# Moving the row variances and scales of a batch behind the queries' low part on VectorE

## The chip, the cores and the metric

The kernel runs on one core of a Trainium2 chip. The time is device microseconds of one execution; the figure compared is the median of the runs shown. In tables and rows PE is TensorE (PEld its weight loads), DVE is VectorE, ACT is ScalarE, POOL is GpSimd, and SP is SyncE, which issues the DMAs.

## What is computed

Two layers of cross attention and a feed-forward mixture of experts, on 4 batches of 512 rows of 256 values, with a context of 4 x 1024 rows of 192. The change touches only the layer norm inside the attention phase, which stands twice in the program (names that begin with `L0a_` and `L1a_`).

```python
def _layernorm(x, axis=-1, eps=1e-05):
    m = jnp.mean(x, axis=axis, keepdims=True)
    v = jnp.var(x, axis=axis, keepdims=True)
    return (x - m) / jnp.sqrt(v + eps)
...
        q = (x @ w_q).reshape(B, Sq, HEADS, DIM_HEAD).transpose(0, 2, 1, 3)
        k = (context @ w_k).reshape(B, Skv, HEADS, DIM_HEAD).transpose(0, 2, 1, 3)
        v = (context @ w_v).reshape(B, Skv, HEADS, DIM_HEAD).transpose(0, 2, 1, 3)
        sim = jnp.einsum('bhid,bhjd->bhij', q, k) * SCALE
        attn = jax.nn.softmax(sim, axis=-1)
        out = jnp.einsum('bhij,bhjd->bhid', attn, v)
        out = out.transpose(0, 2, 1, 3).reshape(B, Sq, INNER)
        return out @ w_o + b_o
...
    x = x + _L0_xattn_ref(_layernorm(x, axis=-1), ctx_768, L0_xattn_w_q, L0_xattn_w_k, L0_xattn_w_v, L0_xattn_w_o, L0_xattn_b_o)
    x = x + _L0_ffn_ref(_layernorm(x, axis=-1), L0_ffn_gate_weight, ...)
```

## The kernel before

An attention phase is 32 segments (`SEGMENTS`), one for each pair of heads of each batch: 8 pairs (`HP`), 4 batches. Segment i takes the exponentials and the product with the values of its own pair; in the same stretch it finishes the pair before it (row sums, normalisation, output product) and prepares the next ones (queries and scores' row maxima of i+1, keys of i+2). Every engine has its own list of instructions, written out by hand in `segment(i)` of that engine, and semaphores tie the lists together. Nothing is reordered by a scheduler, so the order of the code is the order on the engine.

One segment on each engine, in its order:

- TensorE: `transpose_max(i)` (line L802, the first instruction of a segment, which I use as its start), `queries(i+1)`, eight `qk` blocks with quarters of `project_values` between them, `output(i-1)`, then four times `score(i+1, qt)` (L796) with `pv` matmuls (L833) as filling and the keys of i+2 behind the second, and `total(i)` (L845). The third quarter of `project_values` waits for the semaphore `olo`. `score` 1 to 3 and `transpose_max` wait for `max`.
- VectorE: low part of the keys (L521); in segments with i % 8 = 0 or 1 the row statistics (L566); reciprocal of the row sums (L535, PSUM to SBUF), its product with the output (L538), high part (L544) and low part (L548) of the normalised output, of which the last gives `olo`; high part (L504) and low part (L509) of the next queries; in some segments a low part of the rows (L604); two additions of the output to `xres` (L558), four row maxima (L530) which give `max`, with low keys between them.
- GpSimd: `L0a_psums<-L0a_psums,L0a_probs` (L326), 14 sums over the keys' tiles of the exponentials in each segment, both operands in SBUF; low parts of weights (L307, L312) and context (L334).
- ScalarE: exponentials (L400), values (L388), once per batch the square root of the variances (L406, waits for `var`), the normalised rows (L415, waits for `scale`), high parts.

The layer norm of the rows of the next batch, and of the rows that are finished, is spread over the segments of a batch by the step i % 8: statistics in steps 0 and 1, the variances in step 2 (`ROOT`, `variance(b)`, L578 to L583), part of the scales in step 3 (`INNER`, L590 to L592) and the rest in step 4 (`OUTER`, L596 to L598). All of these work on tiles of 128 x 4 or 128 x 8 values in SBUF. L578 to L580 have no wait between them; from L581 on each waits for the one before it (the function `link`).

Of the kernel before, what the change touches and what calls it, by code (L numbers as in the profile page):

```python
# [46 lines left out]
def build(nc, x, ctx_top, ctx_bot, layer_in, out):  # L47
# [6 lines left out]
    with stack:  # L54
# [29 lines left out]
        def bank(n, width=BANK):  # L84
            return psum[:, n * BANK:n * BANK + width]
# [6 lines left out]
        def attention_phase(tag, weights, value_weights, bias, xres, prefetch, source=None, again=False, keep=False, clear=()):  # L92

            with scope() as s:
# [29 lines left out]
                with nc.Block() as block:  # L124
# [38 lines left out]
                    NEXT_STATS, LAST_STATS, ROOT, INNER, OUTER, BIAS = 0, 1, 2, 3, 4, 7  # L163
# [17 lines left out]
                    def columns_of(b):  # L181

                        used = [column for _, column in batches_of(b)] if b >= 0 else [0]
                        return slice(min(used), max(used) + QT)
# [313 lines left out]
                    def _(dve):  # L498
# [7 lines left out]
                        def low_queries(i, heads=(0, 1)):  # L506
                            for h in heads:
                                dve.wait_ge(sem["qhi"], 2 * i + h + 1)
                                last = nc.vector.tensor_tensor(q_lm[0:DH, i % 2, h, :], bank(PLACE["Q"])[HEAD[h], :],  # L509
                                                               q_hh[HEAD[h], i % 2, h, :], ALU.subtract)  # L510
                            if 1 in heads:
                                last.then_inc(sem["qlo"], 1)
# [47 lines left out]
                        def statistics(b, step):  # L560

                            c, column = (b + 1, 0) if step == NEXT_STATS else (b - 1, QT)
                            if step == LAST_STATS:
                                dve.wait_ge(sem["added"], BEFORE + 2 * (b * HP - 1) + 2)
                            for t in range(QT):
                                nc.vector.bn_stats(stats[:, column + t, :], xres[:, c * QT + t, :]).then_inc(sem["stat"], 1)  # L566
                            dve.wait_ge(sem["stat"], counted_stats(b, step))
# [3 lines left out]
                        def link(b, n, ins):  # L571
                            ins.then_inc(sem["link"], 1)
                            dve.wait_ge(sem["link"], LINKS * (b + 1) + n)

                        def variance(b):
                            c = columns_of(b)
                            me, se, mo, so = (stats[:, c, i] for i in (1, 2, 4, 5))
                            nc.vector.tensor_tensor(total_of[:, c], me, mo, ALU.add).then_inc(sem["link"], 1)  # L578
                            nc.vector.tensor_tensor(var[:, c], se, so, ALU.add).then_inc(sem["link"], 1)
                            link(b, 3, nc.vector.tensor_tensor(dif[:, c], me, mo, ALU.subtract))  # L580
                            link(b, 4, nc.vector.scalar_tensor_tensor(dif[:, c], dif[:, c], DIM / 4.0, dif[:, c], ALU.mult, ALU.mult))  # L581
                            link(b, 5, nc.vector.tensor_tensor(var[:, c], var[:, c], dif[:, c], ALU.add))
                            nc.vector.tensor_scalar(var[:, c], var[:, c], 1.0 / DIM, EPS, ALU.mult, ALU.add).then_inc(sem["var"], 1)  # L583

                        def inner_scales(b):
                            c = columns_of(b)
                            dve.wait_ge(sem["sqrt"], b + 2)
                            if b > 0:
                                dve.wait_ge(sem["xn"], 2 * len([i for i in GROUPS if i <= b * HP + INNER]) + 2)
                            link(b, 6, nc.vector.reciprocal(rstd[:, c], std[:, c]))  # L590
                            link(b, 7, nc.vector.tensor_tensor(dif[:, c], var[:, c], rstd[:, c], ALU.mult))
                            link(b, 8, nc.vector.tensor_tensor(dif[:, c], dif[:, c], rstd[:, c], ALU.mult))  # L592

                        def outer_scales(b):
                            c = columns_of(b)
                            link(b, 9, nc.vector.tensor_scalar(dif[:, c], dif[:, c], -0.5, 1.5, ALU.mult, ALU.add))  # L596
                            link(b, 10, nc.vector.tensor_tensor(rstd[:, c], rstd[:, c], dif[:, c], ALU.mult))
                            link(b, 11, nc.vector.scalar_tensor_tensor(shift[:, c], total_of[:, c], -0.5, rstd[:, c], ALU.mult, ALU.mult))  # L598
                            dve.sem_inc(sem["scale"], 1)
# [27 lines left out]
                        def segment(i):  # L627
                            if i + 1 < SEGMENTS:
                                low_keys(i + 1, 1)
                            b, step = divmod(i, HP)  # L630
                            if step == NEXT_STATS and b + 1 < BATCH:
                                if b == 0 and source is not None:
                                    dve.wait_ge(sem["x1"], 16)
                                statistics(b, step)
                            if step == LAST_STATS and b > 0:
                                statistics(b, step)
                            if step == ROOT:
                                variance(b)
                            if step == INNER:
                                inner_scales(b)  # L640
                            if step == OUTER:
                                outer_scales(b)
                            if i == 0:
                                add_bias(0)
                            if step == BIAS and b + 1 < BATCH:
                                add_bias(b + 1)
                            if i > 0:
                                normalise(i - 1)
                            if i > 0:
                                high_output(i - 1)  # L650
                                low_output(i - 1)
                            if i + 1 < SEGMENTS:
                                high_queries(i + 1)
                                low_queries(i + 1)
                            if i > 0:
                                if i in GROUPS:
                                    low_rows(number(i), GROUPS[i][0], PLACE["XT"])
                                add_output(i - 1)
                            if i + 1 < SEGMENTS:
                                for qt in range(QT):  # L660
                                    maximum(i + 1, qt)
                                    if qt in (1, 2) and i + 2 < SEGMENTS:
                                        low_keys(i + 2, 0, (qt - 1,))
# [1100 lines left out]
```

## Time and profile before

| what | value |
|---|---|
| median of 3 runs (2613.11 to 2613.93) | 2613.51 us |
| the profiled execution: time, span | 2618.82 us, 2616.9 us |
| TensorE busy | 2520.7 us, 96% of the span |
| VectorE busy | 2091.2 us, 80% |
| GpSimd busy | 1482.1 us, 57% |
| ScalarE busy | 1246.1 us, 48% |
| mean granted TensorE clock | 0.985 of full speed |

The profile is one execution with an instruction record for each engine. The profiled execution took 2618.82 us, 1.9 us more than its span, and 5.3 us more than the median of the three runs.

### The profile page before, as it was taken

To read this page: it belongs to the slowest core of one execution; us is meant where nothing else is said; L and a number is where in the kernel's file an instruction comes from. 1 tells how busy PE (TensorE), PEld (TensorE's weight loads), DVE (VectorE), ACT (ScalarE), POOL (GpSimd) and SP (SyncE) were. 2 spreads that over 40 slices of the span, in tenths; PEclk is the share of its full clock that TensorE was granted. 3 is DMA by queue.
4 is the path that set the end of the run, shared out by engine and by line. 5 is a ranking of instruction groups with operands and counts; after the bars stand their busy time and mean duration, and the time that the engine had idled before them with its cause. 6 is when DMAs were issued, how large, how long until landed. Compare 5 with 4: busy or idle time off the path is not lost. (4 is left out here: it accounts for less than half of the span.)

```text
span 2616.9 us, 37958 instructions
## 1 busy us (share of the span) xinstructions
PE 2520.7 (96%) x13304; PEld 1776.5 (68%) x13304; DVE 2091.2 (80%) x2602; ACT 1246.1 (48%) x1774; POOL 1482.1 (57%) x1124
## 2 busy tenths in 40 slices
PE   8999999999999889999999899999999999998795
PEld 6666565656665678888888766666666665656684
DVE  7888888888888487777777788888888888866695
ACT  5555555555554323333333355455555454533393
POOL 5878777877777311111111187687878777760345
PEclk9999999999999999999999999999999999999897
DMA  4122212222221200000000121222131222115112
GB/s 147 45 59 53 63 45 58 63 49 50 63 51 41 72 19 24 24 24 24 24 24 18 47 75 45 55 61 59 45 79 45 59 53 55 45 29 235 47 54 88
DMA packets 118648, 145.09 MB, mean 55 GB/s; under 512 B 63856, under 2 KB 80112, under 8 KB 117488
## 3 DMA queue, kind: packets, MB, share of 16 engines
q1 hardware_dynamic: 113664, 136.10, 19.3%
q0 software_dynamic: 1536, 4.20, 0.5%
q10 hardware_dynamic: 3312, 3.02, 0.3%
q8 instruction: 81, 1.33, 0.2%
q14 instruction: 55, 0.45, 0.1%
HBM read 80.93 MB, written 11.80 MB: 35 GB/s over the span
## 5 line engine op out<-in xcount | busy, mean ns | idle before, releaser
L326 POOL TENSOR_TENSOR L1a_psums<-L1a_psums,L1a_probs 128x512 f32<-128x512 f32 x384 | 479.1, 1293 | 0.0
L326 POOL TENSOR_TENSOR L0a_psums<-L0a_psums,L0a_probs 128x512 f32<-128x512 f32 x384 | 478.8, 1289 | 0.0
L530 DVE TENSOR_REDUCE L1a_row_max<-psum 128x2 f32<-128x2048 f32 x128 | 293.6, 2293 | 59.2 <-PE psum L796 58.9
L530 DVE TENSOR_REDUCE L0a_row_max<-psum 128x2 f32<-128x2048 f32 x128 | 293.5, 2293 | 57.7 <-PE psum L796 57.2
L400 ACT ACTIVATE L0a_probs<-psum 128x1024 f32<-128x1024 f32 x256 | 251.6, 1027 | 105.9 <-PE psum L819 105.7
L400 ACT ACTIVATE L1a_probs<-psum 128x1024 f32<-128x1024 f32 x256 | 251.6, 1027 | 105.1 <-PE psum L819 104.9
L1168 DVE SCALAR_TENSOR_TENSOR xres<-psum,L0e_weights_of,xres 128x256 f32<-128x256 f32 x544 | 225.6, 478 | 22.6 <-PE psum L1379 21.7
L833 PE MATMUL psum<-L1a_probs,L1a_v 128*64 128x512 f32 x1024 | 240.5, 601 | 0.0
L833 PE MATMUL psum<-L0a_probs,L0a_v 128*64 128x512 f32 x1024 | 240.4, 601 | 0.0
L1365 PE MATMUL psum<-xnT_hi,L0e_w_hi 128*128 128x512 f32 x544 | 215.0, 395 | 9.4 <-DVE L0e_hid L1176 9.4
L1365 PE MATMUL psum<-xnT_lo,L0e_w_hi 128*128 128x512 f32 x544 | 214.6, 394 | 0.0
L1365 PE MATMUL psum<-xnT_hi,L0e_w_lo 128*128 128x512 f32 x544 | 213.1, 392 | 0.0
L818 PE MATMUL psum<-L0a_q_hh,L0a_k_st 128*128 128x512 f32 x512 | 204.4, 399 | 1.4 <-ACT L0a_probs L400 0.9
L818 PE MATMUL psum<-L1a_q_hh,L1a_k_st 128*128 128x512 f32 x512 | 204.3, 399 | 1.4 <-ACT L1a_probs L400 0.9
L819 PE MATMUL psum<-L1a_q_lm,L1a_k_hs 65*128 65x512 f32 x512 | 203.1, 397 | 0.0
L819 PE MATMUL psum<-L0a_q_lm,L0a_k_hs 65*128 65x512 f32 x512 | 203.0, 397 | 0.0
L1113 ACT ACTIVATE L0e_act_g<-psum 128x512 f32<-128x512 f32 x136 | 81.3, 598 | 243.4 <-PE psum L1365 243.4
L558 DVE TENSOR_TENSOR xres<-psum,xres 128x512 f32<-128x512 f32 x128 | 88.6, 692 | 114.9 <-PE psum L708 113.8
L1176 DVE TENSOR_TENSOR L0e_hid<-psum,L0e_act_g 128x512 f32<-128x512 f32 x136 | 93.7, 689 | 102.8 <-ACT L0e_act_g L1113 102.7
L326 POOL TENSOR_TENSOR L1a_psums<-L1a_probs 128x512 f32<-128x512 f32 x64 | 82.4, 1307 | 153.5 <-ACT L1a_probs L400 153.5
L1087 POOL TENSOR_TENSOR L0e_w_lo<-L0e_raw,L0e_w_hi 128x768 fp32r<-128x768 f32 x16 | 30.0, 1875 | 242.1 <-ACT L0e_w_hi L1102 242.1
L1087 POOL TENSOR_TENSOR L0e_w_lo<-ctx_stage,L0e_w_hi 128x768 fp32r<-128x768 f32 x16 | 30.6, 1914 | 240.9 <-ACT L0e_w_hi L1102 240.9
(384 smaller groups left out, 6148.6 us busy)
## 6 DMA issues: line engine op xcount, KB each, us to landing
L0a_k_hs<-L0a_k_st SPq DMA_DIRECT2D x64, 256.0 KB, 3.6
L1a_k_hs<-L1a_k_st SPq DMA_DIRECT2D x64, 256.0 KB, 3.7
L0a_raw<-in_attention SPq DMA_DIRECT2D x33, 384.0 KB, 3.4
L1a_raw<-in_attention SPq DMA_DIRECT2D x33, 384.0 KB, 3.4
L1weights<-in_sorted SPq DMA_DIRECT2D x2, 6144.0 KB, 20.6
L0a_q_hh<-L0a_q_hh SPq DMA_DIRECT2D x64, 128.0 KB, 2.3
L1a_q_hh<-L1a_q_hh SPq DMA_DIRECT2D x64, 128.0 KB, 2.3
ctx_stage<-in_experts SPq DMA_DIRECT2D x19, 384.0 KB, 3.0
```

Of the source, the lines that this page charges most:

```text
L326: nc.gpsimd.tensor_tensor(psums[:, h, :], a, probs[:, h, kv, :], ALU.add).then_inc(sem["acc"], 1)
L400: nc.scalar.activation(probs[:, h, 2 * kp:2 * kp + 2, :], slot(h).rearrange("p (n q) -> p n q", n=2), ACT.Exp, scale=SCALE)\
L530: nc.vector.reduce_max(row_max[:, qt, 0:33:32], psum[:, 0:4 * BANK].rearrange("p (h k) -> p h k", h=2), axis=AX.X).then_inc(sem["max"], 1)
L558: nc.vector.tensor_tensor(rows, bank(PLACE[f"OUT{half}"]), rows, ALU.add).then_inc(sem["added"], 1)
L818: nc.tensor.matmul(dst, k_st[:, par, h, keys_of], q_hh[:, par, h, :], start=True, stop=False)
L819: last = nc.tensor.matmul(dst, k_hs[0:DH + 1, par, h, keys_of], q_lm[0:DH + 1, par, h, :], start=False, stop=True)
L833: last = nc.tensor.matmul(O[HEAD[h], :], v[:, pair % 2, kv, cols], probs[:, h, kv, :], start=kv == 0, stop=kv == KVT - 1)
L1087: nc.gpsimd.tensor_tensor(w_lo[:, par, :], raw[par], w_hi[:, par, :], ALU.subtract)\
L1113: nc.scalar.activation(act_g[:, u % 2, :], bank(u % 2), ACT.Silu).then_inc(sem["silu"], 1)
L1168: last = nc.vector.scalar_tensor_tensor(acc, bank(4 + 2 * (u % 2) + n // 2)[:, (n % 2) * DIM:(n % 2 + 1) * DIM], weights_of[:, ds(j * (2 * ...
L1176: nc.vector.tensor_tensor(hid[:, u % 2, :], bank(2 + u % 2), act_g[:, u % 2, :], ALU.mult)\
L1365: last = nc.tensor.matmul(bank(2 * g + u % 2), a[:, par, w], m[:, kd, rows], start=n == 0, stop=n == 3 * KD - 1)
```

## The change

The three calls of `segment(i)` on VectorE move from in front of `normalise(i - 1)` to behind `low_queries(i + 1)`. Nothing is added or removed, and the lists of the other four engines and of the DMA queues are the same row for row.

```diff
@@ -634,12 +634,6 928.27 0.51 PE L1365 MATMUL psum<-xnT_hi,L0e_w_hi 128*128 128x512 f32 x1 [2.67 <-DVE L0e_hid L1176]
...
929.00:932.00 3.00, 3.00 (x9) 0.50 0.00 0
                                 statistics(b, step)
                             if step == LAST_STATS and b > 0:
                                 statistics(b, step)
-                            if step == ROOT:
-                                variance(b)
-                            if step == INNER:
-                                inner_scales(b)
-                            if step == OUTER:
-                                outer_scales(b)
                             if i == 0:
                                 add_bias(0)
                             if step == BIAS and b + 1 < BATCH:
@@ -652,6 +646,12 928.27 0.51 PE L1365 MATMUL psum<-xnT_hi,L0e_w_hi 128*128 128x512 f32 x1 [2.67 <-DVE L0e_hid L1176]
...
929.00:932.00 3.00, 3.00 (x9) 0.50 0.00 0
                             if i + 1 < SEGMENTS:
                                 high_queries(i + 1)
                                 low_queries(i + 1)
+                            if step == ROOT:
+                                variance(b)
+                            if step == INNER:
+                                inner_scales(b)
+                            if step == OUTER:
+                                outer_scales(b)
                             if i > 0:
                                 if i in GROUPS:
                                     low_rows(number(i), GROUPS[i][0], PLACE["XT"])
```

On VectorE, segment 10 of the first attention phase (step 2, `ROOT`), before:

```order
L521 TENSOR_TENSOR L0a_k_st<-psum,L0a_k_st 64x512 x2
L578 TENSOR_TENSOR L0a_total_of<-L0a_stats 128x8
L579 TENSOR_TENSOR L0a_var<-L0a_stats 128x8
L580 TENSOR_TENSOR L0a_dif<-L0a_stats 128x8
L581 SCALAR_TENSOR_TENSOR L0a_dif<-L0a_dif 128x8
L582 TENSOR_TENSOR L0a_var<-L0a_var,L0a_dif 128x8
L583 TENSOR_SCALAR L0a_var<-L0a_var 128x8
L535 RECIPROCAL L0a_inv<-psum 128x512
L538 TENSOR_TENSOR psum<-psum,L0a_inv 128x512
L544 CAST L0a_o_split<-psum 128x512
L548 TENSOR_TENSOR L0a_o_split<-psum,L0a_o_split 128x512
```

The same place on VectorE in the changed kernel, down to the output's additions:

```order
L535 RECIPROCAL L0a_inv<-psum 128x512
L538 TENSOR_TENSOR psum<-psum,L0a_inv 128x512
L544 CAST L0a_o_split<-psum 128x512
L548 TENSOR_TENSOR L0a_o_split<-psum,L0a_o_split 128x512
L504 CAST L0a_q_hh<-psum 64x512 x2
L509 TENSOR_TENSOR L0a_q_lm<-psum,L0a_q_hh 64x512 x2
L578 TENSOR_TENSOR L0a_total_of<-L0a_stats 128x8
L579 TENSOR_TENSOR L0a_var<-L0a_stats 128x8
L580 TENSOR_TENSOR L0a_dif<-L0a_stats 128x8
L581 SCALAR_TENSOR_TENSOR L0a_dif<-L0a_dif 128x8
L582 TENSOR_TENSOR L0a_var<-L0a_var,L0a_dif 128x8
L583 TENSOR_SCALAR L0a_var<-L0a_var 128x8
```

The six instructions of `variance` have changed places with the six rows from the reciprocal to the queries' low part; L558 follows them directly.

On VectorE, segment 12 (step 4, `OUTER`) in the changed kernel:

```order
L548 TENSOR_TENSOR L0a_o_split<-psum,L0a_o_split 128x512
L504 CAST L0a_q_hh<-psum 64x512 x2
L509 TENSOR_TENSOR L0a_q_lm<-psum,L0a_q_hh 64x512 x2
L596 TENSOR_SCALAR L0a_dif<-L0a_dif 128x8
L597 TENSOR_TENSOR L0a_rstd<-L0a_rstd,L0a_dif 128x8
L598 SCALAR_TENSOR_TENSOR L0a_shift<-L0a_total_of,L0a_rstd 128x8
L558 TENSOR_TENSOR xres<-psum,xres 128x512 x2
```

Before, L596 to L598 stood in front of the reciprocal L535. Segment 11 (step 3) is moved in the same way with L590 to L592. There are 4 segments of each of these steps in an attention phase, so 8 of each in the program.

## Rows read from the trace of the kernel before

**Rows 1.** Timeline of TensorE: start, duration, instruction; first instruction of segments 9, 10, 11

```profile
271.31 0.30 PE L802 MATMUL psum<-ident,L0a_row_max 128*33 128x128 f32 x1
...
297.56 0.30 PE L802 MATMUL psum<-ident,L0a_row_max 128*33 128x128 f32 x1
...
324.60 0.30 PE L802 MATMUL psum<-ident,L0a_row_max 128*33 128x128 f32 x1
```

**Rows 2.** Waits of TensorE for L548: total us, times, longest us

```profile
PE psum L708 <- DVE L0a_o_split L548: 3.2, 5, 1.1
...
PE psum L708 <- DVE L1a_o_split L548: 1.6, 3, 0.6
```

**Rows 3.** Timeline of VectorE in segments 10 and 12 of the first phase

```profile
298.69 1.49 DVE L578 TENSOR_TENSOR L0a_total_of<-L0a_stats 128x8 f32<-128x8 f32 x1
...
300.18 0.16 DVE L580 TENSOR_TENSOR L0a_dif<-L0a_stats 128x8 f32<-128x8 f32 x1
...
300.98 3.36 DVE L535 RECIPROCAL L0a_inv<-psum 128x512 f32<-128x512 f32 x1
...
307.87 1.39 DVE L509 TENSOR_TENSOR L0a_q_lm<-psum,L0a_q_hh 64x512 fp32r<-64x512 f32 x2
...
352.38 0.17 DVE L598 SCALAR_TENSOR_TENSOR L0a_shift<-L0a_total_of,L0a_rstd 128x8 f32<-128x8 f32 x1
352.69 3.36 DVE L535 RECIPROCAL L0a_inv<-psum 128x512 f32<-128x512 f32 x1
```

**Rows 4.** Timeline of GpSimd in segment 10

```profile
298.30 1.84 POOL L307 TENSOR_TENSOR L0a_w_split<-L0a_raw,L0a_w_split 128x768 fp32r<-128x768 f32 x1
...
303.82 14.97 POOL L326 TENSOR_TENSOR L0a_psums<-L0a_psums,L0a_probs 128x512 f32<-128x512 f32 x12
...
305.08 2.53 POOL L326 TENSOR_TENSOR L0a_psums<-L0a_psums,L0a_probs 128x512 f32<-128x512 f32 x2
```

**Rows 5.** Timeline of VectorE in segment 9, with idle time and what ended it

```profile
283.60 1.40 DVE L558 TENSOR_TENSOR xres<-psum,xres 128x512 f32<-128x512 f32 x2 [1.44 <-PE psum L708]
...
288.37 2.29 DVE L530 TENSOR_REDUCE L0a_row_max<-psum 128x2 f32<-128x2048 f32 x1 [1.10 <-PE psum L796]
```

**Rows 6.** Timeline of TensorE in segment 9, second and third scores

```profile
287.60 0.73 PE L796 MATMUL psum<-L0a_k_st,L0a_q_hh 64*128 64x512 f32 x4
...
290.78 0.73 PE L796 MATMUL psum<-L0a_k_st,L0a_q_hh 64*128 64x512 f32 x4
```

**Rows 7.** Timelines of VectorE and GpSimd where both have operands in SBUF

```profile
38.47 1.90 DVE L624 TENSOR_TENSOR xres<-xres,L0a_bias_sb 128x1024 f32<-128x1024 f32 x1
...
39.24 2.27 POOL L326 TENSOR_TENSOR L0a_psums<-L0a_probs 128x512 f32<-128x512 f32 x1
...
929.69 2.98 POOL L1087 TENSOR_TENSOR L0e_w_lo<-ctx_stage,L0e_w_hi 128x768 fp32r<-128x768 f32 x1 [19.34 <-ACT L0e_w_hi L1102]
...
929.69 0.69 DVE L1181 TENSOR_TENSOR L0e_hid_lo<-L0e_hid,L0e_hid_hi 128x512 fp32r<-128x512 f32 x1
930.29 0.69 DVE L1208 TENSOR_TENSOR L0e_gt<-L0e_choice,L0e_late 128x512 f32<-128x512 f32 x1
931.02 2.20 DVE L1209 TENSOR_TENSOR L0e_eq<-L0e_choice,L0e_late 128x512 f32<-128x512 f32 x1
...
9.68 1.30 POOL L348 TENSOR_TENSOR ctx_lo<-ctx_stage,ctx_hi 128x512 fp32r<-128x512 f32 x1 [7.99 <-ACT ctx_hl L435]
...
9.78 1.36 DVE L675 TENSOR_SCALAR L0a_probs<-xres,L0a_rstd,L0a_shift 128x256 f32<-128x256 f32 x1
```

**Rows 8.** TensorE idle, and the next windows' granted clock (third column)

```profile
928.27 0.51 PE L1365 MATMUL psum<-xnT_hi,L0e_w_hi 128*128 128x512 f32 x1 [2.67 <-DVE L0e_hid L1176]
...
929.00:932.00 3.00, 3.00 (x9) 0.50 0.00 0
...
916.96 0.50 PE L1365 MATMUL psum<-xnT_hi,L0e_w_hi 128*128 128x512 f32 x1 [1.34 <-DVE L0e_hid L1176]
...
917.00:918.00 1.00, 1.00 (x5) 1.00 0.00 0
```

## The prediction

> **What bounds the kernel now.** I first read the starts of the segments on TensorE. A usual segment, such as number 9, takes 297.56 - 271.31 = 26.25 us; segment 10, a step 2 (ROOT), takes 324.60 - 297.56 = 27.04 us [rows 1]. A ROOT segment loses 0.79 us. The waits say where, and they are short: TensorE is the bound, and what stops it counts in full. It waits for `olo` (L548) 5 times in the first phase and 3 times in the second [rows 2]; one of the five, the longest at 1.1 us, lies at the phase's end, and the others average (3.2 - 1.1)/4 = 0.53 us and 1.6/3 = 0.53 us. That is 7 stalls for 8 ROOT segments. The recorded idle time is less than what the segment loses, because the end of the matmul ahead is drawn long; I use the 0.79.
>
> The cause is on VectorE. In segment 10 `variance` lies from 298.69 to 300.98, 2.29 us, of which the first instruction, L578, alone takes 1.49; L580, of the same kind and size, takes 0.16 [rows 3]. What holds it is GpSimd: its L307 runs from 298.30 to 300.14, and L578 ends at 300.18 [rows 3, 4].
>
> **What the move takes away.** In a ROOT segment L535 to L548 begin 2.29 us earlier, far more than the stall, so it goes. 7 x 0.79 = 5.5 us are won. In steps 3 and 4 there is no stall to remove; their reciprocal comes earlier for nothing. GpSimd, ScalarE and SP keep their order; the copies of the queries can only start earlier.
>
> **What it costs at the new place.** In what follows t is the time from a segment's start. L509 ends in segment 10 at 307.87 + 1.39 = 309.26, t = 11.70 [rows 3]; without `variance` ahead it ends at t = 9.41. Next comes L558, which waits for TensorE's output and starts in a segment without a stall at 283.60 - 271.31, t = 12.29 [rows 5]. So there is a hole of 2.88 us. Unhindered, the six instructions take 2.29 - (1.49 - 0.16) = 0.96 us and would vanish in it, and steps 3 and 4, with three each, all the more. Even held by one GpSimd instruction as before, 2.29 fits.
>
> But GpSimd is otherwise occupied there. Before, after L307 it has nothing until its sums begin. At t = 9.4 it is in the middle of its sums: 12 of them in 14.97 us, one every 1.25 us without a gap, and one ends at 305.08 + 2.53 = 307.61, t = 10.05 [rows 4]; the next at 11.30, 12.55, 13.80. What a VectorE instruction with two SBUF operands does then is seen at two places [rows 7]. L624 (38.47) lasts 1.90 us and lies across the end of a sum; the next sum, begun at 39.24, lasts 2.27 instead of 1.25 to 1.3 and ends at 41.51, 1.14 us after L624. So one holds the other off, and each gets its turn where the other ends. And at 929.69 GpSimd's L1087 and VectorE's L1181 start together; L1208 follows L1181 with overlap at 930.29, undisturbed at 0.69; then L1209, which starts 0.04 us behind L1208's end, takes 2.20, until 933.22, while L1087 ends at 932.67. So VectorE instructions that follow each other without a wait pass in one turn, but after a gap of 0.04 us GpSimd goes first.
>
> In `variance` L578, L579 and L580 have no wait between them; L581, L582 and L583 each wait for the one before. I therefore take four turns. In segment 10 L578 ended 0.04 us after GpSimd's L307 (300.18 after 300.14) and L580 0.20 after it (300.34) [rows 3, 4]. So L578 to L580 wait for the sum that ends at t = 10.05 and are through by 10.25. The next sum ends 1.14 us after that, at 11.39, as behind L624, and L581 0.04 later, at 11.43; then one sum's 1.25 us for each: L582 12.68, L583 13.93. L558 starts 0.03 behind, at 13.96 instead of 12.29, 1.67 us late.
>
> Does L583 wait too? It has one tensor. L675 of the same operation (1.36 us, 9.78 to 11.14) ended just behind GpSimd's L348 (10.98) [rows 7], so I take it that it does, less surely at 4 or 8 values. The Trainium skill ("VectorE: DVE Perf Modes", Mode 2×_2P) says that such an operation with SBUF operands may use both read ports; the trace agrees through L675, and by that page L583 waits.
>
> What L558 is late, the first maximum is late: it stands right behind L558, which ends at 283.60 + 1.40 = 285.00, and with the 2.29 us of the second maximum it ends at 287.29. The second score starts at 287.60, 0.31 us behind; the second maximum ends at 288.37 + 2.29 = 290.66 and the third score starts 0.12 behind [rows 5, 6]. So 0.12 us is enough for the semaphore, and the first pair has about 0.2 us to spare. 1.67 - 0.20 = 1.47 us goes to TensorE, which has no other work queued ahead of the score. Everything behind it, scores, keys, the next segment, moves by that. 8 x 1.47 = 11.8 us.
>
> Step 4: L596 (tensor scalar) gets through at 10.09, L597 at 11.34, L598 at 12.59, L558 0.14 later at 12.73, as L535 started 0.14 behind L598's end (352.55, 352.69) [rows 3]. 0.44 - 0.20 = 0.24, times 8 is 1.9 us. Step 3: L590, a reciprocal of one tensor, runs at once, L591 is through by 10.09, L592 by 11.34: nothing. If L590 waits too, it is like step 4.
>
> Hidden in all this: GpSimd is pushed back by some tenths of a us per segment, and its sums, which end at 303.82 + 14.97 = 318.79, are needed only for L845 just ahead of the next segment's start at 324.60 [rows 1, 4]. ScalarE's root gets `var` at about t = 13.9; it has only key and weight work behind it, which waits for TensorE, late itself.
>
> **Sum.** -5.5 + 11.8 + 1.9 = +8.2 us. The profiled execution, 2618.8 us (span 2616.9 and 1.9 around it), would become 2627.0; it ran 5.3 us over the median of the three runs, and on that the same sum gives 2613.5 + 8.2 = 2621.7. 0.2%, about what a measurement tells from no change, is 5.2 us; both +8.2 and the gain alone lie near it.
>
> **The rivals.**
>
> A. *Each of the six takes a turn.* If L579 and L580 lose their turn like L581, L583 ends at 10.09 + 5 x 1.25 = 16.3, L558 is 4.1 late, TensorE 3.9: 8 x 3.9 + 1.9 - 5.5 = +27.6 us. Then the clock comes in. After TensorE's idle 2.67 us at 928.27 the granted clock was 0.50 in the next windows for 3 us, so 1.5 us of work is lost; after 1.34 us idle it stayed 1.00 [rows 8]. With stalls of 3.9 that is up to 8 x 1.5 = 12 more, +39.6. For it: `variance`'s instructions are tiny. Against it: L1208 passed with L1181. The Trainium skill ("SBUF — State Buffer", Who interferes with whom) has the pair of ports as a lock held for one whole instruction, with the other blocked; by its word alone the lock would be free between L578 and L579. 12%.
>
> B. *L583 and L596 do not wait.* Then L583 follows L582 by 0.2 and ends at 12.9 in ROOT, L558 is 0.6 late, 0.4 at TensorE; step 4 is hidden: 8 x 0.4 - 5.5 = -2.3 us, 2611.2. For it: 4 to 8 values and not 256. 17%.
>
> C. *The other side: the small instructions pass between the sums.* If GpSimd does not get in between the links, or tiny instructions hardly hold each other, `variance` ends one wait and its own 0.96 later, by t = 11.1, inside the hole, and nothing remains of the cost: -5.5 us, 2608.0, faster by 0.21%. It decides near t = 13.2: there L558 is 0.9 late, TensorE 0.7, and the 5.5 us won are used up; only an end before 12.5 keeps all of them. For it: the hole of 2.88 and the visible stall. Against it: L578's 1.49. 13%.
>
> D. *My chain, with the clock dropping at the 1.5 us stalls too.* 8 x 1.5 = 12 more: +20.2. Against it: 1.34 us of idle did nothing [rows 8]. 8%.
>
> My forecast has 50%, from +5 to +11: 0.3 us in the place where a sum ends moves it by 2.4.
>
> **Chances.** Slower by over 0.2%: forecast (most of it), A and D, 0.63. Faster: most of C, and only just, 0.08. Within: B, the rest, 0.29. The range from 2607.5 to 2635 holds the forecast, B, C and D and leaves out A.
>
> **What would show it.** In ROOT segments of the changed kernel: no idle time before L708 from `olo`; L578 about 0.7 us long, L581, L582 and L583 each about 1.1 to 1.3 instead of 0.17; L558 without idle ahead of it and at t = 13.9; TensorE idle about 1.5 us before its second score; segments of 26.25 + 1.5 = 27.7 us instead of 27.04. In step 4 L596 to L598 long, and segments of 26.4 to 26.5. GpSimd's sums between them 0.1 longer. If L581 to L583 keep 0.17, C is right; if L583 alone does, B; if L579 and L580 are stretched, A.
>
> I would be wrong most easily in how many turns there are, since each costs 8 x 1.25 = 10 us.

## The result, and the profile after

The changed kernel takes 2651.56 us (median of 4 runs, 2647.12 to 2654.93), the kernel before 2613.31 us (4 runs, 2611.55 to 2613.93): ratio 1.0146, 95% interval 1.0129 to 1.0164. It is slower by 38 us. I had forecast 2621.7 with a range up to 2635, so the time lies outside the range; it lies at rival A, every instruction of `variance` a turn and the clock on top, for which I had worked out +39.6 us and given 12%.

(In the diff of the section on the change, the two hunk headings have taken up rows of [rows 8] by a slip. They do not belong to the diff.)

The profiled execution took 2654.93 us, span 2652.9, at a mean granted clock of 0.978. On its page, busy time by engine, TensorE is now busier than in the table of before by 13.6 us, VectorE by 65.5, and GpSimd by nothing:

```profile
PE 2534.3 (96%) x13304; PEld 1786.8 (67%) x13304; DVE 2156.7 (81%) x2602; ACT 1245.3 (47%) x1774; POOL 1480.9 (56%) x1124
```

TensorE does the same 13304 instructions. Busier with the same work means a lower clock, and VectorE's 65.5 us more on the same 2602 instructions means that some of them are held while they count as running.

First the starts of segments 10 and 11 on TensorE in the changed kernel (start, duration, instruction), which answer to [rows 1]:

```profile
304.48 0.30 PE L802 MATMUL psum<-ident,L0a_row_max 128*33 128x128 f32 x1
...
336.89 0.30 PE L802 MATMUL psum<-ident,L0a_row_max 128*33 128x128 f32 x1
```

Segment 10 takes 32.41 us instead of 27.04. Read in the same way, the eight ROOT segments take 31.21 to 32.68 us. They sum to 254.06 us after and 215.52 before, +38.5; the eight step 4 segments sum to 210.3 instead of 8 x 26.24 = 209.9, +0.4. The whole loss of 38 us lies there. (The spans of the two profiled executions differ by 36.0. The 2.9 us less lie outside these segments: the changed kernel's execution takes 2.7 us more ahead of the first segment, 0.7 more between the phases and 6.2 less behind the second. The stretch behind the last takes about 282 us in some profiled executions of these kernels and 287 to 290 in others, the kernel before among them; I haven't traced why.)

The timeline of VectorE in segment 10 of the changed kernel answers to [rows 3]:

```profile
313.92 0.65 DVE L578 TENSOR_TENSOR L0a_total_of<-L0a_stats 128x8 f32<-128x8 f32 x1
314.50 1.31 DVE L579 TENSOR_TENSOR L0a_var<-L0a_stats 128x8 f32<-128x8 f32 x1
315.74 1.33 DVE L580 TENSOR_TENSOR L0a_dif<-L0a_stats 128x8 f32<-128x8 f32 x1
317.11 1.20 DVE L581 SCALAR_TENSOR_TENSOR L0a_dif<-L0a_dif 128x8 f32<-128x8 f32 x1
318.34 1.20 DVE L582 TENSOR_TENSOR L0a_var<-L0a_var,L0a_dif 128x8 f32<-128x8 f32 x1
319.57 1.20 DVE L583 TENSOR_SCALAR L0a_var<-L0a_var 128x8 f32<-128x8 f32 x1
320.80 1.29 DVE L558 TENSOR_TENSOR xres<-psum,xres 128x512 f32<-128x512 f32 x2
```

And GpSimd's at the same time, which answers to [rows 4]:

```profile
310.74 14.88 POOL L326 TENSOR_TENSOR L0a_psums<-L0a_psums,L0a_probs 128x512 f32<-128x512 f32 x12
```

The six instructions end at 314.57, 315.81, 317.07, 318.31, 319.54 and 320.77, so 1.23 to 1.26 us apart. GpSimd's sums come every 14.88/12 = 1.24 us. L578 waits for the rest of the running sum (0.65 us), and each of the five behind it, of 8 values a partition, for one whole sum, L579 and L580 too, which have no semaphore wait ahead of them. The other seven ROOT segments show the same times within 0.02 us. L558 begins at t = 320.80 - 304.48 = 16.32 instead of 12.29 [rows 5], with no idle time ahead of it.

TensorE in the same segment, its second score, with its idle time and what ended it, answers to [rows 6]:

```profile
324.35 1.22 PE L796 MATMUL psum<-L0a_k_st,L0a_q_hh 64*128 64x512 f32 x4 [3.52 <-DVE L0a_row_max L530]
```

It starts at t = 19.87 instead of 287.60 - 271.31 = 16.29 in [rows 6], 3.58 us late. The same four matmuls take 1.22 us instead of 0.73. Why they do stands in the granted clock around them. The windows of TensorE (start and end, length, busy time and instructions, granted clock, DMA share, GB/s):

```profile
320.50:322.50 2.00, 0.33 (x2) 1.00 0.01 4
322.50:324.30 1.80, 0.00 (x0) 0.74 0.00 0
324.30:329.30 5.00, 4.96 (x13) 0.50 0.07 4
...
330.30:336.00 5.70, 5.70 (x30) 1.00 0.48 99
```

The clock is at 1.00 when TensorE goes idle, falls within the idle time, and then stays at 0.50, that is at 1.2 instead of 2.4 GHz, for 5 us and more of full work before it is back at 1.00. Windows of 1 us behind the same stall of the other seven ROOT segments reach 0.50 too; it lasts about 3 us of work in five of the eight and about 6 in three. The list of waits of TensorE says that this is the rule in every ROOT segment (total us, times, longest); no wait for L530 stood in this list before, and the waits for `olo` [rows 2] are gone but for 0.4 us at a phase's end:

```profile
PE psum L796 <- DVE L0a_row_max L530: 14.1, 4, 3.5
PE psum L796 <- DVE L1a_row_max L530: 14.1, 4, 3.5
...
PE psum L708 <- DVE L0a_o_split L548: 0.4, 1, 0.4
```

Last, step 4 in segment 12 of the changed kernel, VectorE's timeline:

```profile
372.57 0.65 DVE L596 TENSOR_SCALAR L0a_dif<-L0a_dif 128x8 f32<-128x8 f32 x1
373.26 1.20 DVE L597 TENSOR_TENSOR L0a_rstd<-L0a_rstd,L0a_dif 128x8 f32<-128x8 f32 x1
374.50 1.22 DVE L598 SCALAR_TENSOR_TENSOR L0a_shift<-L0a_total_of,L0a_rstd 128x8 f32<-128x8 f32 x1
375.93 1.29 DVE L558 TENSOR_TENSOR xres<-psum,xres 128x512 f32<-128x512 f32 x2 [0.21 <-DVE L0a_shift L598]
```

### The profile page after: what moved, and what is told of

Read it like the earlier page. It is cut to its first block and busy times, and to the rows that moved or that the text cites. A ratio compares the mean times of both kernels' runs of the same rounds, so it can differ in the third digit from the quotient of the medians.

```text
span 2652.9 us, 37950 instructions
## 1 busy us (share of the span) xinstructions
PE 2534.3 (96%) x13304; PEld 1786.8 (67%) x13304; DVE 2156.7 (81%) x2602; ACT 1245.3 (47%) x1774; POOL 1480.9 (56%) x1124
## 3 DMA queue, kind: packets, MB, share of 16 engines
q8 instruction: 81, 1.33, 0.2%
## 5 line engine op out<-in xcount | busy, mean ns | idle before, releaser
L530 DVE TENSOR_REDUCE L0a_row_max<-psum 128x2 f32<-128x2048 f32 x128 | 293.4, 2292 | 62.7 <-PE psum L796 62.1
L530 DVE TENSOR_REDUCE L1a_row_max<-psum 128x2 f32<-128x2048 f32 x128 | 293.4, 2292 | 60.6 <-PE psum L796 60.0
L326 POOL TENSOR_TENSOR L1a_psums<-L1a_probs 128x512 f32<-128x512 f32 x64 | 82.3, 1306 | 154.0 <-ACT L1a_probs L400 154.0
L326 POOL TENSOR_TENSOR L0a_psums<-L0a_probs 128x512 f32<-128x512 f32 x64 | 82.3, 1306 | 147.2 <-ACT L0a_probs L400 147.2
```

Of the source, the lines that this page charges most:

```text
L326: nc.gpsimd.tensor_tensor(psums[:, h, :], a, probs[:, h, kv, :], ALU.add).then_inc(sem["acc"], 1)
L530: nc.vector.reduce_max(row_max[:, qt, 0:33:32], psum[:, 0:4 * BANK].rearrange("p (h k) -> p h k", h=2), axis=AX.X).then_inc(sem["max"], 1)
```

## The experiments

Ratios are to the kernel before, run on the same chip in the same session. What is named a segment length is read as in [rows 1].

### One half of the change at a time

`var_only` moves only `variance`, `scales_only` only the two calls for steps 3 and 4.

```diff
 # var_only: against the changed kernel
+if step == INNER:
+    inner_scales(b)
+if step == OUTER:
+    outer_scales(b)
 if i == 0:
     add_bias(0)
...
 if step == ROOT:
     variance(b)
-if step == INNER:
-    inner_scales(b)
-if step == OUTER:
-    outer_scales(b)
```

> Only variance (step 2) is moved; inner_scales and outer_scales stay in front of the reciprocal. Theory (variance alone holds up the additions, since each of its six instructions waits for one of GpSimd's sums): within 1 us of the changed kernel in the ROOT segments, 31.2 to 32.7 us each, and +38 us on the kernel before, about 2651. Rival (all three moves share the loss, e.g. through the scales that ScalarE waits for): clearly less, 2630 to 2640.

> Only inner_scales and outer_scales (steps 3 and 4) are moved; variance stays. Theory: L590 does not wait, L591 and L592 end at t = 11.3, L596 to L598 at t = 12.6, so L558 is late by 0.05 and by 0.5 us, of which TensorE feels under 0.1: +0.4 us in all, no measurable change, 2613 to 2615. My recorded price for step 4 was +1.9. Rival (the moved scales share the loss): +5 or more.

Measured: `var_only` 2657.96 against 2619.04, 1.0152 (1.0136 to 1.0168), ROOT segments 31.21 to 32.68 us, TensorE's waits for L530 the same 14.1 and 14.0 us. `scales_only` 2619.47, 1.0003 (0.9994 to 1.0012), step 4 segments 26.27 to 26.33. So `variance` alone carries the loss, and the scales cost nothing that can be timed, though their instructions are held as well.

### Is it GpSimd's sums?

`no_sums` is the changed kernel without the 14 sums of each ROOT segment on GpSimd (the semaphore is counted up in their place); the softmax's row sums of those segments are left out with them.

```diff
+if i % HP == ROOT:
+    pool.sem_inc(sem["acc"], 1)
+else:
+    nc.gpsimd.tensor_tensor(psums[:, h, :], a, probs[:, h, kv, :], ALU.add).then_inc(sem["acc"], 1)
-nc.gpsimd.tensor_tensor(psums[:, h, :], a, probs[:, h, kv, :], ALU.add).then_inc(sem["acc"], 1)
```

> The changed kernel with GpSimd's 14 sums left out in the ROOT segments only (their semaphore steps are given at once, so those segments' row sums are old ones). Theory (GpSimd's operands in SBUF are what holds variance's instructions): L578 to L583 take 0.16 to 0.17 us each, end at t = 10.4, no stall on TensorE, ROOT segments 26.24 us, total before minus 5.6, about 2608. Rival (the new place as such is slow, e.g. waits between VectorE's own instructions): ROOT segments stay over 30 us, about 2651.

Measured: 2613.02 against 2619.04, 0.9981 (0.9971 to 0.999), all ROOT segments 26.24 us. VectorE's timeline in segment 10 (lines shifted by 3: L581 to L586 are the six of `variance`, L561 is the addition):

```profile
306.04 0.17 DVE L581 TENSOR_TENSOR L0a_total_of<-L0a_stats 128x8 f32<-128x8 f32 x1
...
306.82 0.17 DVE L586 TENSOR_SCALAR L0a_var<-L0a_var 128x8 f32<-128x8 f32 x1
...
308.88 1.40 DVE L561 TENSOR_TENSOR xres<-psum,xres 128x512 f32<-128x512 f32 x2 [1.90 <-PE psum L711]
```

Without the sums the six take 306.99 - 306.04 = 0.95 us, as the 0.96 that I had for them unhindered, and 1.90 us of the hole are left. The cost is all the meeting with the sums, and the gain of 8 x (26.94 - 26.24) = 5.6 us is what the removed stall was worth (26.94 is the mean of before's eight).

### How much is stall, how much is clock?

`fill` is the changed kernel with 30 transposes of the identity put on TensorE ahead of the second score of a ROOT segment, so that it works where it had waited.

```diff
 for qt in range(QT):
+    if qt == 1 and i % HP == ROOT:
+        pe.wait_ge(sem["vc"], 2 * i + 6)
+        busy(30, PLACE["K1"])
```

> The changed kernel with 30 transposes of the identity (about 0.12 us each, 3.5 us) on TensorE in front of the second score of each ROOT segment, where it idles 3.5 us, into a bank that is free there. Theory (the stall costs 3.6 us per ROOT segment, and the clock that falls behind the idle time costs 1.4 to 2.8 us more): granted clock stays 1.00, ROOT segments 26.24 + 3.7 = 29.9 us, total 8 x 3.65 - 5.6 = +24 us on before, about 2637. Rival (the clock has its own reason, or the low clock costs nothing): ROOT segments over 31 us, 2650.

Measured: 2639.68 against 2619.04, 1.0083 (1.0068 to 1.0099); ROOT segments 29.80 to 29.84 us, in sum 238.5. TensorE's timeline in segment 10, and its windows with the granted clock in the fourth value:

```profile
316.44 3.50 PE L877 MATMUL psum<-ident 128*128 128x128 f32 x30
320.02 0.73 PE L796 MATMUL psum<-L0a_k_st,L0a_q_hh 64*128 64x512 f32 x4
...
316.00:320.00 4.00, 3.94 (x34) 1.00 0.01 2
320.00:330.00 10.00, 9.97 (x47) 1.00 0.37 81
```

The score is as late as in the changed kernel, but takes 0.73 us again and the clock stays 1.00. So of the +38.5 us in the ROOT segments the stall itself is 238.5 - 209.9 = 28.6 us, the lower clock 254.06 - 238.53 = 15.5 us, and the removed stall -5.6 us. (The medians put the two kernels 38.25 - 20.64 = 17.6 us apart; I go by the segments, since the runs of either kernel scatter by 6 to 8 us.) One idle stretch of 3.5 us costs another 1.9 us on average in slower work behind it.

### Where GpSimd has no sums

`ahead` calls `variance` first of all in a ROOT segment, ahead of `low_keys`, where the sums of the segment have not begun.

```diff
 # ahead: against the kernel before
 def segment(i):
+    b, step = divmod(i, HP)
+    if step == ROOT:
+        variance(b)
     if i + 1 < SEGMENTS:
         low_keys(i + 1, 1)
...
-    if step == ROOT:
-        variance(b)
```

> variance is put in front of low_keys at the start of a ROOT segment, right behind the last row maximum; the scales stay where they were before. There GpSimd is idle until t = 0.74, and variance would run from t = -0.3 to 0.65. Theory: none of its six instructions waits, L548 ends at t = 7.7, before TensorE needs it at 8.2, so the stall of the kernel before goes: ROOT segments 26.24 us, -5.6 us, about 2608, ratio 0.998. Rival (the low keys, now 0.96 us later, hold up TensorE): stalls in front of the key or value products, no gain.

Measured: 2620.47 against 2612.99, 1.0029 (1.002 to 1.0039), a slight loss and not the gain; ROOT segments 28.26 to 28.31, but for the last, 26.24. I had overlooked GpSimd's weight parts. Timeline of VectorE in segment 10, and of GpSimd and TensorE:

```profile
298.04 1.10 DVE L578 TENSOR_TENSOR L0a_total_of<-L0a_stats 128x8 f32<-128x8 f32 x1
299.06 0.16 DVE L579 TENSOR_TENSOR L0a_var<-L0a_stats 128x8 f32<-128x8 f32 x1
299.15 1.82 DVE L580 TENSOR_TENSOR L0a_dif<-L0a_stats 128x8 f32<-128x8 f32 x1
...
297.84 1.27 POOL L312 TENSOR_TENSOR L0a_wv<-L0a_raw_v,L0a_wv 128x512 fp32r<-128x512 f32 x1
299.07 1.87 POOL L307 TENSOR_TENSOR L0a_w_split<-L0a_raw,L0a_w_split 128x768 fp32r<-128x768 f32 x1
...
303.14 0.48 PE L708 MATMUL psum<-L0a_wv,ctx_hi 128*128 128x256 f32 x2 [1.26 <-DVE L0a_k_st L521]
```

L578 waits for L312 and L580 for L307, and the low keys behind them come late for TensorE. L579, in between, passed within 0.16 us, though L307 stood ready just behind L312 (its record begins 0.01 us after L579's): so a VectorE instruction can pass behind the one before it, as L1208 did behind L1181 [rows 7]. It is no rule.

### Half of `variance` at the new place

`split` leaves L578 to L580 in the old place and moves L581 to L583, here L586 to L588.

```diff
 # split: against the kernel before
+def rest_of_variance(b):
+    c = columns_of(b)
     link(b, 4, nc.vector.scalar_tensor_tensor(dif[:, c], dif[:, c], DIM / 4.0, dif[:, c], ALU.mult, ALU.mult))
...
     low_queries(i + 1)
+if step == ROOT:
+    rest_of_variance(b)
```

> L578 to L580 stay in front of the reciprocal, only L581 to L583 move behind the queries' low part. Theory (the cost at the new place is the number of turns, one for each instruction): three turns, ends at t = 12.6, L558 0.4 late, TensorE under 0.1; L578 to L580 still wait for L307, but L548 ends at t = 8.2 - 0.6, so no stall there either: -5 us, about 2608.5. By my recorded reading, in which L578 to L580 share a turn, the three that move would be the whole cost, and this kernel would take about as long as a kernel with four turns less one, also near 2609; the two part at L579 and L580 of the next kernel. Rival (the new place costs whatever stands in it): 2640 and more.

Measured: 2653.51 (5 runs, 2651.68 to 2664.14) against 2612.99, 1.017 (1.0151 to 1.0188). Half the instructions, and it costs as much as all: the interval overlaps that of the changed kernel, and the ROOT segments sum to 257.6 us against its 254.1. The ROOT segments are of two kinds: four of 36.9 to 37.5 us, three of 27.3, and one of 26.25. VectorE in segment 2, GpSimd there, TensorE's second score, and then VectorE in segment 10:

```profile
97.04 10.06 DVE L586 SCALAR_TENSOR_TENSOR L0a_dif<-L0a_dif 128x4 f32<-128x4 f32 x1
107.14 0.16 DVE L587 TENSOR_TENSOR L0a_var<-L0a_var,L0a_dif 128x4 f32<-128x4 f32 x1
...
94.72 12.36 POOL L326 TENSOR_TENSOR L0a_psums<-L0a_psums,L0a_probs 128x512 f32<-128x512 f32 x10
...
111.08 1.22 PE L803 MATMUL psum<-L0a_k_st,L0a_q_hh 64*128 64x512 f32 x4 [8.60 <-DVE L0a_row_max L530]
...
319.11 0.17 DVE L586 SCALAR_TENSOR_TENSOR L0a_dif<-L0a_dif 128x8 f32<-128x8 f32 x1
319.31 1.20 DVE L587 TENSOR_TENSOR L0a_var<-L0a_var,L0a_dif 128x8 f32<-128x8 f32 x1
320.55 1.22 DVE L588 TENSOR_SCALAR L0a_var<-L0a_var 128x8 f32<-128x8 f32 x1
```

In segment 2 one instruction of 4 values a partition is held for 10.06 us. Ten sums of GpSimd run from 94.72 to 107.08 one behind the other, one every 1.24 us; nine of them end while it is held, and it gets through only behind the last, at 107.10. In segment 10 the same line comes 0.13 us ahead of a sum's end and passes in 0.17 us; in that segment of the second phase it comes 0.14 us ahead of one and is held 10.01. So "each gets its turn where the other ends" doesn't hold for every first turn. In the changed kernel L578 got its first turn at the next end in all eight ROOT segments.

### Width, and a semaphore between

`probe` is the kernel `ahead` with three more VectorE instructions with SBUF operands behind the low queries, in steps 2, 3, 4 and 6 of each batch. In step 2 they are tensor tensor of 340, 256, 128 and 64 values in the four batches, with no wait between the three; in step 3 tensor tensor of 8 values, without a wait too; in step 4 those of step 2, each waiting for the one before; and in step 6 tensor scalar of 8 values, each waiting for the one before. (With the additions it is no version of the kernel; 2740.31 us in one run.)

```diff
+for n in range(3):
+    part = mine[:, n * width:(n + 1) * width]
+    if kind % 2 == 0:
+        last = nc.vector.tensor_tensor(part, part, part, ALU.max)
+    elif kind == 1:
+        last = nc.vector.tensor_tensor(small[:, n, :], bias_sb[:, 0:2 * QT], bias_sb[:, 0:2 * QT], ALU.add)
+    else:
+        last = nc.vector.tensor_scalar(small[:, n, :], bias_sb[:, 0:2 * QT], 0.5, 1.0, ALU.mult, ALU.add)
+    last.then_inc(sem["probe"], 1)
+    if kind > 1 or n == 2:
+        dve.wait_ge(sem["probe"], 12 * b + 3 * kind + n + 1)
```

> As the kernel with variance ahead of low_keys, with additional instructions behind the queries' low part that change nothing of the result. Step 2: three tensor_tensor with both operands in SBUF and no wait between them, 128 x 340, 256, 128, 64 values in batches 0 to 3. Step 3: the same with 128 x 8. Step 4: as step 2, each waiting for the one before. Step 6: three tensor_scalar of 128 x 8 in SBUF, each waiting for the one before. Theory (a VectorE instruction keeps GpSimd out only if the next one has been taken up before it ends, which needs a long one): in step 2 the wide ones pass in one turn (second and third at their own length, 0.42 us for 340), the narrow ones and step 3's take a turn each (second and third about 1.3 us); in step 4 all take turns, whatever the width. Rival (every instruction takes a turn, whatever the width): all second and third ones are stretched to about 1.3 us and more. Rival (the two unwaited ones in variance were held by something else): step 3's second and third take 0.16. In step 6 each takes about 1.2 us if a tensor_scalar of 8 values needs the port, 0.17 if not.

Measured, three rows of VectorE's timeline, each of three instructions without a wait between them, and the summary of the two groups of 8 values (min/median/max ns):

```profile
99.46 4.40 DVE L610 TENSOR_TENSOR xres<-xres 128x340 f32<-128x340 f32 x3
...
130.26 3.75 DVE L612 TENSOR_TENSOR L0a_small<-L0a_bias_sb 128x8 f32<-128x8 f32 x3
...
322.44 4.13 DVE L610 TENSOR_TENSOR xres<-xres 128x256 f32<-128x256 f32 x3
...
L612 DVE TENSOR_TENSOR L0a_small<-L0a_bias_sb x12: 152/712/11117, 130.3 to 822.1; 128x8 f32<-128x8 f32 x12
L614 DVE TENSOR_SCALAR L0a_small<-L0a_bias_sb x12: 628/1201/1217, 211.9 to 913.4; 128x8 f32<-128x8 f32 x12
```

Three of 340 values take 4.40 us and three of 8 values 3.75: a turn each, whatever the width and with no semaphore between. The theory that wide instructions pass together and only tiny ones lose the turn falls. L614 shows that a tensor scalar of 8 values waits like the rest. The longest of L612, 11.1 us, is the long hold of `split` again: in four of the eight groups of three (three in the first phase) the first is held so, and the other two then pass in 0.15 us each, since the sums are over. In step 4 it meets two of the eight groups, one of 64 values and one of 256.

### When is one held long?

My next theory was that a first request made near the start of a sum loses again and again. `sweep` takes the steps as in `later` below, where `variance` and the scales are out of the way, and puts one tensor tensor of 8 values at moments that differ from segment to segment, by 0 to 14 tiny reciprocals ahead of it, in steps 1 to 4.

```diff
+if k:
+    for n in range(k):
+        last = nc.vector.reciprocal(small[:, n % 3, n // 3:n // 3 + 1], ones[:, 0:1])
+    last.then_inc(sem["probe"], 1)
+    dve.wait_ge(sem["probe"], 2 * k)
+nc.vector.tensor_tensor(small[:, 3, :], bias_sb[:, 0:2 * QT], bias_sb[:, 0:2 * QT], ALU.add).then_inc(sem["probe"], 1)
```

> The kernel with ROOT, INNER, OUTER = 3, 4, 4, and behind the queries' low part of steps 1 to 4 one additional tensor_tensor of 128 x 8 with both operands in SBUF, put off by 0 to 14 tiny reciprocals of about 0.08 us each, so that it arrives at t = 9.4 to 10.7, over a whole sum of GpSimd. It changes nothing of the result. The two kernels before showed waits of either under 1.5 us or of 10 to 11 us, until GpSimd's sums ended. Theory (who wins at the end of a sum hangs on how the arrival lies to the sum, and who loses once loses until the sums end): the waits are of these two kinds only, the long ones bunched at arrivals from about 0.2 us ahead of a sum's start to 0.15 behind it. Rival (fair turns with rare accidents): long ones spread over all arrivals, or waits between 1.5 and 10 us.

Measured (one run, 2857.4 us), the summary of the group in the first phase and two of its rows:

```profile
L611 DVE TENSOR_TENSOR L0a_small<-L0a_bias_sb x15: 273/9870/11102, 97.7 to 917.8; 128x8 f32<-128x8 f32 x15
...
97.70 0.65 DVE L611 TENSOR_TENSOR L0a_small<-L0a_bias_sb 128x8 f32<-128x8 f32 x1
...
125.08 10.58 DVE L611 TENSOR_TENSOR L0a_small<-L0a_bias_sb 128x8 f32<-128x8 f32 x1
```

Of 30 such instructions 7 were held under 1 us and 23 for 9.4 to 11.1 us, until GpSimd's sums were over; none lies in between. But the long ones are not those near a sum's start: one that came at t = 11.03 in the first phase was held 10.15 us, its fellow at 11.02 in the second 0.31, and one that came in the middle of a sum (10.58) 10.6 in both. The theory of the moment within a sum falls. Something coarser is left in the record: the four that came at t = 9.44 and 9.82, while GpSimd's fifth sum ran, all got in at its end, and of the 26 that came from t = 10.06 on 23 were held. The tiny reciprocals ahead, with SBUF operands too, took 141 to 166 ns throughout and were not held.

### Two ways out

`hold` is the changed kernel in which GpSimd waits ahead of its sixth sum of a ROOT segment until `variance` is through. `later` is the kernel before with the steps renumbered, so that `variance` falls into step 3 and both scales into step 4, at the old place, where GpSimd has nothing at the time.

```diff
 # hold
+if i % HP == ROOT and n == 5:
+    pool.wait_ge(sem["var"], i // HP + 2)
 # later
-NEXT_STATS, LAST_STATS, ROOT, INNER, OUTER, BIAS = 0, 1, 2, 3, 4, 7
+NEXT_STATS, LAST_STATS, ROOT, INNER, OUTER, BIAS = 0, 1, 3, 4, 4, 7
```

> The changed kernel, and in ROOT segments GpSimd waits for variance's end in front of its sixth sum (the one that would start at t = 10.02). Theory (L578 to L583 are held by GpSimd's queued sums alone): L578 waits until 10.05, the other five take 0.16 each, variance ends at t = 10.9, inside the hole; GpSimd's sums end 0.9 later, at 22.1, before they are needed; ROOT segments 26.24 us, 5.6 below before, ratio 0.998. Rival (handing the port over costs time by itself, or the sums' delay is felt at the segment's end): ROOT segments 27 us or more.

> The kernel before with the constants ROOT, INNER, OUTER = 3, 4, 4 for 2, 3, 4: variance in front of the reciprocal of step 3, where GpSimd has nothing between t = 0 and 3.76, and all scales in front of that of step 4. Theory (place decides by what GpSimd does there): variance's six instructions take 0.16 each, L548 ends by t = 7.7 in step 3 and 8.0 in step 4, TensorE needs it at 8.2: no stall in any segment, 5.6 below before, ratio 0.998. Rival (the stall of step 2 only moves to step 3 or 4): no change.

Measured side by side, against 2611.7: `hold` 2608.32, 0.9986 (0.9977 to 0.9996), and `later` 2606.1, 0.9979 (0.9969 to 0.9988). In both, the ROOT segments take 26.24 to 26.25 us. VectorE and GpSimd in `hold` (L580 to L585 are `variance`):

```profile
305.92 0.64 DVE L580 TENSOR_TENSOR L0a_total_of<-L0a_stats 128x8 f32<-128x8 f32 x1
...
307.16 0.17 DVE L585 TENSOR_SCALAR L0a_var<-L0a_var 128x8 f32<-128x8 f32 x1
308.77 1.40 DVE L560 TENSOR_TENSOR xres<-psum,xres 128x512 f32<-128x512 f32 x2 [1.43 <-PE psum L710]
...
307.80 5.00 POOL L328 TENSOR_TENSOR L0a_psums<-L0a_psums,L0a_probs 128x512 f32<-128x512 f32 x4 [1.28 <-ACT L0a_probs L402]
```

And VectorE in `later`, segment 11, the first and last of `variance`:

```profile
324.63 0.17 DVE L578 TENSOR_TENSOR L0a_total_of<-L0a_stats 128x8 f32<-128x8 f32 x1
...
325.40 0.17 DVE L583 TENSOR_SCALAR L0a_var<-L0a_var 128x8 f32<-128x8 f32 x1
```

With one pause of 1.28 us in GpSimd's row the change does what its place promised: only the first instruction waits, for the rest of the running sum (0.64), and the five behind it pass in 0.16 to 0.17 each. (The row names ScalarE's L402 for the pause; the wait that the edit puts there is for L585, which ends at 307.33, 0.47 us ahead of the sum.) `later` has the lowest median and needs no pause; its interval overlaps that of `hold`, so between the two nothing is decided. Both beat the kernel before, by little, and the changed kernel clearly.

## Why the prediction was wrong, point by point

- **The removed stall.** Right. I put -5.5 us on it; `no_sums` shows -5.6, and the wait for L548 is gone from the ROOT segments.
- **The hole and the steps behind it.** Right. L509 ends and L578 begins at t = 9.44, the hole ends at 12.29. L558 4.03 us late made the second score 3.58 us late, where I had reckoned with 0.2 us to spare and hence 3.83; it was 0.25 too much, of which L558 made up 0.11 by running without a wait inside (1.29 instead of 1.40 us).
- **"VectorE instructions that follow each other without a wait pass in one turn, but after a gap of 0.04 us GpSimd goes first. ... I therefore take four turns."** This step failed. All six took a turn of their own, L578 the rest of the running sum (0.65 us) and the five behind it 1.20 to 1.33 us each, and `probe` shows it for instructions from 8 to 340 values with no wait between. I had made a rule from one row, L1208 behind L1181 [rows 7]. There GpSimd's instruction was one that had waited for its data and began together with L1181, not one of a row of sums. `ahead` has the same exception at L579. The two missed turns moved the stall from a forecast 8 x 1.47 = 11.8 us to the measured 28.6.
- **The clock.** I had it only in rivals A and D. 1.34 us of idle time had left it at 1.00 and 2.67 had not [rows 8]; a stall of 3.5 us brought it to 0.50 in all eight segments. I had put at most 8 x 1.5 = 12 us on it for A; `fill` shows 15.5, since in three of the eight it stayed low for about 6 us of work and not for the 3 us that I had read. With my four turns the stall would have been 1.47 us, and this term nil as far as the rows tell: seven stalls of 1.2 to 1.3 us in `ahead` left the clock at 1.00 too.
- **L583 and L596 wait.** Right: tensor scalar of 8 values was held like the others (1.20 and 0.65 us, and L614 in `probe`). That was my point against rival B, which is out. The Trainium skill ("VectorE: DVE Perf Modes", Mode 2×_2P), which I had named for it, says only that such an operation may use both read ports; that it waits, even at 8 values, is what these rows show.
- **Step 4.** The mechanism was right, the size not: I had +1.9 us, the eight segments show +0.4, and `scales_only` 1.0003. L596 got in at t = 10.09 as forecast and L558 0.21 us behind L598, 0.51 us late, of which TensorE felt 0.05. So the first pair had about 0.45 us to spare and not 0.20; the ROOT segments give the same, 4.03 - 3.58. **Step 3** cost nothing, as I said; L590 was not held.
- **Rival C** (tiny instructions slip between the sums) is out by the same rows; it holds only where GpSimd makes a pause, and `hold` shows that.
- **Sum by measured terms:** -5.6 + 28.6 + 15.5 + 0.4 = +38.9 us in the segments, against +38.25 between the medians. Forecast: -5.5 + 11.8 + 0 + 1.9 = +8.2. That rival A's +39.6 comes so near is partly luck: its stall was 2.6 us too large and its price for step 4 1.5, and its clock was 3.5 too small.

The chance of 12% for rival A was too small for another reason as well: the rule on which it rested had a page behind it. The Trainium skill ("SBUF — State Buffer", Who interferes with whom) has the shared ports as a lock held for one whole instruction; I had read out of it, which it doesn't say, that between two instructions the lock is free for whoever asks. `probe` agrees for every width tried (4.40 us for three of 340 values). What that section doesn't lead one to expect is the hold over a whole row of sums in `split`.

**What stays open.** What decides whether a VectorE instruction gets in at the next end of a sum or is held until the sums are over. In the changed kernel none was held longer than 1.34 us; in `split`, `probe` and `sweep` many were. Neither the width nor the moment within a sum explains it. What the traces do show is a border: of the first requests of a segment, all 37 that came before t = 9.9, while the fifth sum ran (24 in the changed kernel, 8 in `probe`, 4 in `sweep`, 1 in `split`), got in at its end, and of the 57 that came from t = 10.05 on 33 were held until the sums were over (23 of 26 in `sweep`, 4 of 7 in `split`, 6 of 24 in `probe`). Why, no run shows; the changed kernel, whose requests begin at t = 9.44, was on the good side of it. That a request made directly behind a turn already won gets the next one fits the changed kernel and `probe`, but it was only argued, and no run isolates it. The same goes for L1208 and for L579 in `ahead`, which passed.

## What to carry to other kernels

Each VectorE instruction with two operands in SBUF, and a tensor scalar on SBUF too, that falls among GpSimd's SBUF instructions without a gap between them should be costed as one whole GpSimd instruction, whatever its size (here 1.2 to 1.3 us for 8 values that alone take 0.17), and it may be held until GpSimd's row of them ends. Count the instructions and not their bytes; put such small work where GpSimd is idle (`later`, 0.9979), or let GpSimd wait once (`hold`, 0.9986), and don't take a hole on VectorE for free time before having looked at what GpSimd does in it. A new stall on TensorE must be priced with the slower clock behind it, here 28.6 us of waiting and 15.5 of slower work.

## What the runs showed of the hardware that I had not expected

- A VectorE instruction of 4 values was held 10.06 us while nine GpSimd sums ended (`split`); in `sweep` 23 of 30 were held 9.4 to 11.1 us and 7 under 1 us, with none between.
- VectorE instructions of 8 to 340 values without a wait between them don't share a turn (3.75 us for three of 8, 4.13 for three of 256, 4.40 for three of 340).
- Reciprocals with SBUF operands were not held among the same sums: 105 of them in each phase took 141 to 166 ns.
- After 3.5 us without work TensorE ran at a granted clock of 0.50 for 3 to 6 us of work, at a cost of 1.9 us on average; 30 transposes of the identity in the gap kept it at 1.00.
